# Division on coefficients, output bias in the rows' biases, and LayerNorm's factor and shift inside a gelu on features, between graph attention layers

## The reference, cut to what matters

```python
def _layer_norm(x, g, b):
    mu = jnp.mean(x, axis=-1, keepdims=True)
    var = jnp.var(x, axis=-1, keepdims=True)
    return g * (x - mu) / jnp.sqrt(var + 1e-05) + b

def _gatv2(h, src, dst, n, Wl, bl, Wr, br, att, bias):
    H, C = att.shape
    xl = (h @ Wl + bl).reshape(n, H, C)
    xr = (h @ Wr + br).reshape(n, H, C)
    x_i = xl[dst]
    x_j = xr[src]
    e = jax.nn.leaky_relu(x_i + x_j, NEG_SLOPE)
    logit = jnp.einsum('ehc,hc->eh', e, att)
    m = jax.ops.segment_max(logit, dst, num_segments=n)
    ex = jnp.exp(logit - m[dst])
    den = jax.ops.segment_sum(ex, dst, num_segments=n)
    alpha = ex / (den[dst] + 1e-16)
    out = jax.ops.segment_sum(alpha[..., None] * x_j, dst, num_segments=n)
    return out.reshape(n, H * C) + bias
...
for Wl, bl, Wr, br, att, bo, g, be in layers:
    h_new = jax.nn.gelu(_layer_norm(_gatv2(h, src, dst, n, Wl, bl, Wr, br, att, bo), g, be), approximate=False)
    h = h + h_new if h.shape == h_new.shape else h_new
out = h @ W_out + b_out
```

## Time and profile before

| what | value |
|---|---|
| median of 3 runs | 6894.73 us (6893.92 to 6904.86) |
| the profiled execution's own time | 6896.92 us |
| its span, first to last instruction | 6894.9 us |
| mean granted TensorE clock | 0.790 of full speed |
| PE busy | 4310.3 us, 63% |
| POOL busy | 4046.8 us, 59% |
| DVE busy | 3609.1 us, 52% |
| ACT busy | 1561.5 us, 23% |

### The profile page before, as it was taken

How to read it: one execution, slowest core, us unless ns; L and a number is a source line. 1 busy time by engine, 2 the same in 40 slices (tenths; PEclk the granted TensorE clock), 3 DMA queues, 4 the chain that set the end, 5 groups by cost and what they waited for, 6 DMA issues and landing times. The chain is left out here.

```text
span 6894.9 us, 131457 instructions
## 1 busy us (share of the span) xinstructions
PE 4310.3 (63%) x28719; PEld 3668.6 (53%) x28720; DVE 3609.1 (52%) x9059; ACT 1561.5 (23%) x3121; POOL 4046.8 (59%) x3272
## 2 busy tenths in 40 slices
PE   6768874666666636666665366666653656565664
PEld 5765333555555535555555365555553355555554
DVE  7888235455545565555555655555556244444445
ACT  4664100111111101111111011111111044444442
POOL 0100004888888548888884488888840078888883
PEclk9989986787778868888777688887876877787777
DMA  5753442666666526666665366666641311111111
GB/s 149 201 163 115 114 116 75 172 184 179 180 176 180 160 75 176 183 177 183 176 180 153 80 180 184 178 182 181 179 138 46 106 40 41 41 41 41 41 42 26
DMA packets 767773, 902.49 MB, mean 131 GB/s; under 512 B 278082, under 2 KB 543484, under 8 KB 767662
## 3 DMA queue, kind: packets, MB, share of 16 engines
q10 hardware_dynamic: 272511, 333.81, 16.8%
q1 hardware_dynamic: 234670, 326.01, 16.2%
q0 software_dynamic: 260480, 241.33, 15.3%
HBM read 654.18 MB, written 243.02 MB: 130 GB/s over the span
## 5 line engine op out<-in xcount | busy, mean ns | idle before, releaser
L484 POOL DMA_INDIRECT rows<-row_table,now x2400 | 2975.9, 1240 | 1646.2 <-issue 1588.9
L484 POOL DMA_INDIRECT rows<-node_table,now x800 | 1022.3, 1278 | 674.5 <-issue 668.5
L722 PE MATMUL zp<-parts,hot_t 125*125 x8100 | 755.2, 251 | 824.0 <-issue 570.6
L803 DVE SCALAR_TENSOR_TENSOR z<-zp,own 125x512 f32<-125x512 f32 x672 | 464.6, 691 | 1413.5 <-PE zp L725 1339.2
L722 PEld LDWEIGHTS zp<-parts,hot_t 125*125 125x125 bf16 x8100 | 698.0, 158 | 907.5 <-issue 903.0
L725 PE MATMUL zp<-rows,ident 125*125 x2700 | 941.4, 481 | 164.8 <-SPq L506 163.9
L736 PEld LDWEIGHTS sums<-values,hot 125*125 125x125 f32 x5376 | 877.4, 223 | 114.9 <-issue 42.7
L651 ACT CAST hot<-hot 125x500 f32<-125x500 bf16 x672 | 408.5, 608 | 2235.5 <-DMA hot<-hots 1262.6
L736 PE MATMUL sums<-values,hot 125*125 125x137 f32 x5376 | 879.5, 315 | 41.1 <-DVE values L815 36.4
L725 PEld LDWEIGHTS zp<-rows,ident 125*125 125x125 f32 x2700 | 553.8, 228 | 255.2 <-issue 178.8
L972 PE MATMUL turn<-ident,onehot 125*126 125x125 f32 x904 | 178.8, 333 | 515.0 <-DVE onehot L540 497.5
(11 more groups left out here) (414 smaller groups left out, 5047.6 us busy)
## 6 DMA issues: line engine op xcount, KB each, us to landing
back<-gathered ACTq DMA_DIRECT2D x624, 231.0 KB
gathered<-rows SPq DMA_DIRECT2D x600, 231.0 KB
hot_t<-hots_t ACTq DMA_DIRECT2D x678, 122.1 KB
hot<-hots ACTq DMA_DIRECT2D x672, 122.1 KB
counts<-pairs SPq DMA_DIRECT2D x75, 685.1 KB
rows<-row_table,now POOLq DMA_INDIRECT x2400
spread_slots<-slot_table POOLq DMA_DIRECT2D x56, 488.3 KB
hots_t<-hot_t SPq DMA_DIRECT2D x112, 218.8 KB
```

Source lines behind the costliest of these rows:

```text
L484: pool.indirect_dma_start(rows[:, q, j, :], None, table, bass.IndirectOffsetOnAxis(ap=now[:, half, lane + j:lane + j + 1], axis=0)).then_i ...
L722: pe.matmul(zp[:, p, j, 0:ROW], hot_t[:, q, j * P:(j + 1) * P], own[part], start=part == 0 and j % 2 == 0, stop=False, skip_group_check=True)
L803: dve.scalar_tensor_tensor(out=z[:, p, :, :], in0=zp[:, p, :, 0:D], scalar=0.0, in1=rows_of(own_att, HALF), op0=ALU.max, op1=ALU.mult).the ...
```

## The change

The functions `load`, `attention`, `linear_nodes` and the loops stay as they are. The change has four parts.

- The reciprocal of the denominator multiplies the two coefficients (`es`, 100 values a partition each) ahead of the scaling, not the result (3200 values a partition) behind it.
- The output bias is added to `xr`'s bias and subtracted from `xl`'s at the start of `attention_rows` (two DVE instructions of 125x128). The attention weights of a node sum to one, so its sum over rows carries the bias, and `xl + xr` in the logits is what it was. The bias comes as a new tile `late` with the layer's other loads.
- `normalize` and `to_features` become one block, `normalize_to_features`: DVE does (y - mean) * rstd in one pass, PE transposes each group of four windows when it is scaled, and ACT reads the PSUM bank with gelu, with the gain as per-partition scale and the shift as per-partition bias, since features are partitions now. In the first layer ACT writes `ft` itself; in the others it writes `grown`, and DVE adds it to `ft` group by group, two groups behind.
- `h` on nodes is gone as a tile. Gain and shift are loaded as columns (128 partitions x 4 bytes) instead of broadcasts; after the last layer `xr`'s memory serves as `h`.

The core of the diff:

```diff
+def normalize_to_features(nc, g, y, gain, shift, func, dst, onto=False):
...
+            def add_on(q):
+                dve.wait_ge(activated, q + 1)
+                dve.tensor_tensor(dst[:, part(q)], dst[:, part(q)], grown[:, part(q)], ALU.add)
...
+            link(dve.reciprocal(rstd[:, :], std[:, :]))
+            for q in range(GROUPS):
+                for w in windows(q):
+                    dve.tensor_scalar(y[:, w, :], y[:, w, :], moments[:, w, 0:1], rstd[:, w:w + 1], ALU.subtract, ALU.mult).then_inc(scaled, 1)
+                if onto and q >= 2:
+                    add_on(q - 2)
+            if onto:
+                for q in range(GROUPS - 2, GROUPS):
+                    add_on(q)
...
+            for q in range(GROUPS):
+                pe.wait_ge(scaled, windows(q)[-1] + 1)
+                for w in windows(q):
+                    ins = pe.transpose(bank[:, q, (w % 4) * P:(w % 4 + 1) * P], y[:, w, :], g.ident[0:P, 0:P])
+                ins.then_inc(turned, 1)
...
+            for q in range(GROUPS):
+                act.wait_ge(turned, q + 1)
+                act.activation(grown[:, part(q)], bank[:, q, 0:span(q)], func, bias=shift, scale=gain).then_inc(activated, 1)
...
+            link(dve.tensor_tensor(bias[:, 0, 0:D], bias[:, 0, 0:D], late[:, :], ALU.subtract))
+            link(dve.tensor_tensor(bias[:, 1, 0:D], bias[:, 1, 0:D], late[:, :], ALU.add))
...
+                (late[:, :], a[f"L1_gnn_bo{i}"].partition_broadcast(P))]
...
-                    link(dve.tensor_tensor(heads(xr[:, :, 0:D]), heads(xr[:, :, 0:D]), over(m[:, :, :]), ALU.mult))
-                    link(dve.tensor_tensor(xr[:, :, 0:D], xr[:, :, 0:D], rows_of(bo, WIN), ALU.add))
+                    for n in range(2):
+                        link(dve.tensor_tensor(es[:, :, n, :], es[:, :, n, :], m[:, :, :], ALU.mult))
...
-            def keep(dve, link):
-                if i == 0:
-                    link(dve.tensor_copy(h[:, :, :], xr[:, :, 0:D]))
-                else:
-                    link(dve.tensor_tensor(h[:, :, :], h[:, :, :], xr[:, :, 0:D], ALU.add))
-
-            normalize(nc, xr[:, :, 0:D], g.eps, gain=gain, shift=shift, func=ACT.Gelu, after=keep)
-            to_features(nc, g.ident, h, D, ft)
+            normalize_to_features(nc, g, xr[:, :, 0:D], norm[:, 0:1], norm[:, 1:2], ACT.Gelu, ft, onto=i > 0)
```

More of the change, by code:

```diff
@@ L305, in _ @@
                     act.activation(y[:, w:w + FIVE, :], y[:, w:w + FIVE, :], func).then_inc(activated, 1)
+def normalize_to_features(nc, g, y, gain, shift, func, dst, onto=False):
+    with Scope(nc) as sc:
+        stats = sc.sb("stats", [P, WIN, 6])
+        moments = sc.sb("moments", [P, WIN, 2])
+        std = sc.sb("std", [P, WIN])
+        rstd = sc.sb("rstd", [P, WIN])
+        grown = sc.sb("grown", [D, N]) if onto else dst
+        bank = sc.ps("bank", [128, GROUPS, 512])
+        names = ("step", "stats_ready", "moments_ready", "std_ready", "scaled", "turned", "activated")
+        step, stats_ready, moments_ready, std_ready, scaled, turned, activated = (sc.sem(x) for x in names)
+        block = sc.block()
+        part = lambda q: slice(4 * q * P, 4 * q * P + span(q))
+        @block.vector
+        def _(dve):
+            link = Link(dve, step)
+            def add_on(q):
+                dve.wait_ge(activated, q + 1)
+                dve.tensor_tensor(dst[:, part(q)], dst[:, part(q)], grown[:, part(q)], ALU.add)
+            for w in range(WIN):
+                dve.bn_stats(stats[:, w, :], y[:, w, :]).then_inc(stats_ready, 1)
+            dve.wait_ge(stats_ready, WIN)
+            for w in range(WIN):
+                dve.bn_aggr(moments[:, w, :], stats[:, w, :]).then_inc(moments_ready, 1)
+            dve.wait_ge(moments_ready, WIN)
+            dve.wait_ge(std_ready, 1)
+            link(dve.reciprocal(rstd[:, :], std[:, :]))
[7 more added lines that the diff above has]
+                    add_on(q)
+        @block.tensor
+        def _(pe):
+            for q in range(GROUPS):
[3 more added lines that the diff above has]
+                ins.then_inc(turned, 1)
+        @block.scalar
+        def _(act):
+            act.wait_ge(moments_ready, WIN)
+            act.activation(std[:, :], moments[:, :, 1], ACT.Sqrt, bias=g.eps[0:P, :]).then_inc(std_ready, 1)
+            for q in range(GROUPS):
+                act.wait_ge(turned, q + 1)
+                act.activation(grown[:, part(q)], bank[:, q, 0:span(q)], func, bias=shift, scale=gain).then_inc(activated, 1)
@@ L2010, in layer0, with attention_rows @@
         normalize(nc, x[:, :, :], g.eps, before=lambda dve, link: link(dve.tensor_tensor(x[:, :, :], x[:, :, :], cur[:, :, :], ALU.add)))
-def attention_rows(nc, g, i, k, ft, w, att_w, bias, own, table, xr, xl, loads):
+def attention_rows(nc, g, i, k, ft, w, att_w, bias, late, own, table, xr, xl, loads):
     per = 3
@@ L2072, in layer_loads @@
                 (att_w[:, :], a[f"L1_gnn_att{i}"].rearrange("h c -> (h c)").partition_broadcast(D)),
-                (bias[:, 0, 0:D], a[f"L1_gnn_bl{i}"].partition_broadcast(P)), (bias[:, 1, 0:D], a[f"L1_gnn_br{i}"].partition_broadcast(P))]
+                (bias[:, 0, 0:D], a[f"L1_gnn_bl{i}"].partition_broadcast(P)), (bias[:, 1, 0:D], a[f"L1_gnn_br{i}"].partition_broadcast(P)),
+                (late[:, :], a[f"L1_gnn_bo{i}"].partition_broadcast(P))]
     with Scope(nc) as sc:
-        h = sc.sb("h", [P, WIN, D])
         ft = sc.sb("ft", [128, N])
@@ L2083, in layer1 @@
         own = sc.sb("own", [P, D])
-        row = sc.sb("row", [P, 3, D])
+        late = sc.sb("late", [P, D])
+        norm = sc.sb("norm", [D, 2])
         ls = sc.sb("ls", [P, WIN, HEADS])
@@ L2098, in layer1 @@
             k = HID if i == 0 else D
-            rows = [(row[:, n, :], a[f"L1_gnn_{v}{i}"].partition_broadcast(P)) for n, v in enumerate(("bo", "g", "be"))]
-            bo, gain, shift = (row[:, n, :] for n in range(3))
-            attention_rows(nc, g, i, k, ft, w, att_w, bias, own[:, :], table, xr, xl, rows)
+            cols = [(norm[:, n:n + 1], column(a[f"L1_gnn_{v}{i}"])) for n, v in enumerate(("g", "be"))]
+            attention_rows(nc, g, i, k, ft, w, att_w, bias, late, own[:, :], table, xr, xl, cols)
             attention(nc, g, table, xl, xr, att_w[0:P, :], own[:, :], spill, ls)
@@ L2129, in _ @@
                     dve.wait_ge(exped, 1)
-                    link(dve.tensor_tensor(heads(xr[:, :, 0:D]), heads(xr[:, :, 0:D]), over(es[:, :, 0, :]), ALU.mult))
-                    link(dve.tensor_tensor(heads(g.acc[:, :, 0:D]), heads(g.acc[:, :, 0:D]), over(es[:, :, 1, :]), ALU.mult))
-                    link(dve.tensor_tensor(xr[:, :, 0:D], xr[:, :, 0:D], g.acc[:, :, 0:D], ALU.add))
                     link(dve.tensor_tensor(m[:, :, :], es[:, :, 1, :], g.acc[:, :, D:D + HEADS], ALU.mult))
```

8 lines of the change are left out of this document (6 added, 2 removed).

## The result

| | kernel before | changed kernel |
|---|---|---|
| median of 4 runs each | 6897.28 us (6893.92 to 6904.86) | 6853.16 us (6848.78 to 6855.49) |
| ratio | | 0.9934, 95% interval 0.9917 to 0.9951 |
| the profiled execution, and its span | 6896.92, 6894.9 us | 6855.44, 6853.7 us |
| mean granted TensorE clock | 0.790 | 0.794 |

The changed kernel is 44 us faster, where 57 were forecast. 6853.2 lies 1.2 us above the upper end of the forecast range. The forecast counted from 6894.7, the median of three executions; a fourth moved that median to 6897.3. 44.1 us less than 6894.7 would be 6850.6, inside the range.

What follows compares the result with a forecast made beforehand. DVE, busy almost without a gap between barriers in the parts between edge loops, was taken as the bound. Terms -19.4 + 1.9 + 0.4 - 15.4 - 13.5 - 13.3 + 2.0 = -57.3 from 6894.7 gave 6837.4 us, range 6829 to 6852.

Steps and rivals of the forecast that it cites:

- Division and bias: Block combining the sums: two large DVE instructions go, two small come, -19.4 us over three layers; bias instructions +1.9, load +0.4.
- One pass and gelu on features: First scaling to next block: 8.7, 11.1 and 11.1 us in the three layers, gains 15.4, 13.5 and 13.3 us.
- the rival *mode: Scaling pass reads one tensor and streams twice as fast: 5.2 us less, 6832.2 us; chance 0.04.
- The last additions: Second and third layer, additions of gelu results to `ft`: only the last ones wait, under 0.5 us.
- The clock: After spurts of transposes `linear_nodes` begins at PE's low clock level, +2.0 us; the two `attention_rows` 0.
- The rival *the clock: PE stays at the low level throughout `linear_nodes` and `attention_rows`: +11.8 us, 6849.2 us; chance 0.10.
- Lockstep: Normalisation, second and third layer: each group costs its whole chain of 3.4 us, +26 us, 6863 us; chance 0.03.
- slower gathers: Edge loops: moved `attention` tiles slow all 2400 gathers by 38 ns, +91 us, 6929 us; chance 0.03.
- no effect: Parts between loops: something else holds the barrier and the change saves nothing, 6894 us; chance 0.02.
- the loops over edges within 1 us of before: Sign to check: edge loops keep their length within 1 us; a change of several us would make the prediction wrong.
- theory C: Edge loops, posed for the follow-up runs: they lengthen whenever the parts are shorter, giving back 8 to 12 us.
- B: Edge loops, posed for the follow-up runs: they scatter by some us between executions, whatever the kernel, by either sign.

Runs made afterwards that it cites:

- c_after: The changed kernel again on another chip, quad number read as the lower 16 bits of its word; 7045.01 us, ratio 0.9932 to the kernel before.
- f_after: The changed kernel a third time, on the last chip, with the same 16-bit quad read; 7051.49 us, ratio 0.9932 to the kernel before.
- f_short_after: The changed kernel without its three long attention edge loops, two fills in their place; 2963.10 us, against 3014.56 for the kernel before cut likewise.
- d_warm: The changed kernel plus spare PE transposes in the holes between groups and at the start of each `attention_rows`; ratio 0.9934 to the kernel before.
- c_: Runs on one chip: control, changed kernel, changed kernel with tiles at old addresses, division-only edit; the kernel before took 7096.09 us there.
- d_: Runs on another chip: kernel before with only the bias edit (1.0002), changed kernel with spare transposes (0.9934) or with sums on POOL (0.9924).
- c_coeff: The kernel before with only the division moved to the coefficients; ratio 0.9993 to the kernel before, three parts 9.0 us less than the control.
- f_best: The changed kernel with next-layer sums prepared on POOL and three spare transposes behind groups 2 to 4 of later layers; 7047.84 us, ratio 0.9919.
- d_pool: The changed kernel with the next `attention_rows`' bias instructions, logit sums and scaled weights moved to POOL during normalisation; ratio 0.9924 to the kernel before.

## Why the prediction was right, and where not

From `some` behind a loop to the end of the part, in four profiles of the changed kernel's parts (`changed`, `c_after`, `f_after`, `f_short_after`), in us:

| step | forecast | before | found |
|---|---|---|---|
| block that combines the sums, each layer | -6.46 | 21.58 | 15.12, in all (-6.46) |
| first scaling to next block, 1st layer | 8.7 | 24.17 | 8.86, 8.41, 8.40, 8.40 |
| the same, 2nd layer | 11.1 | 24.57 | 11.21, 11.22, 11.21, 11.21 |
| the same, 3rd layer | 11.1 | 24.41 | 11.21, 11.22, 11.21, 11.21 |
| `linear_nodes` | +2.0 | 6.71 | 8.30, 8.60, 8.29, 9.46 (+1.6 to +2.8) |
| second and third `attention_rows` (first three profiles) | +0.65 each | 21.60, 20.29 | 22.37, 22.10; 21.63, 21.65; 21.58, 22.03 |

- **Division and bias: right.** The load stayed hidden. `late` was issued at 2418.08 + 0.34 and SP waited 3.8 us for it, so it was there near 2422, 8 us before DVE's last instruction ends (the first line is from SP's timeline, the second from its waits in that block):

```profile
2418.08 0.34 SPq L2175 DMA_DIRECT2D late<-in_L_gnn_bo  x1
...
SPq L103 <- DMA late<-in_L_gnn_bo: 3.8, 1, 3.8
```

  The two bias instructions take 0.32 us each. The column loads cost nothing visible.
- **One pass and gelu on features: right.** The tails came out 0.3 us short of the forecast or 0.15 over it in the first layer and 0.1 over it in the others. The two values of the first layer come from TensorE's clock: over the last transposes it was 0.50 in the changed kernel and 0.80 in `c_after`, and the last group's gelu takes 0.45 us and not 0.36. Of the two rules weighed, the first falls at this size: 25 instructions of L340 take 6.50 us, 0.26 each, about as long as the two-tensor form. "VectorE: DVE Perf Modes" of the Trainium skill, in "The perf-mode tier table", gives fp32 tensor_scalar twice the rate of tensor_tensor, for 2048 elements; with 128 elements the trace does not show it. So the rival *mode* is out. The other holds: L361 takes 767 ns. "ScalarE: Activation LUTs" of the Trainium skill, in "What ACT_TABLE_LOAD costs", has 93 ns for each pointer operand, which on top of the 677 ns of the row with one gives an estimate of 0.77 us; the trace agrees. My 0.7 was the row with one pointer.

```profile
L361 ACT ACTIVATE grown<-bank,norm x14: 449/767/768, 3794.5 to 5155.5; 128x500 f32<-128x500 f32 x12, 128x125 f32<-128x125 f32 x2
```

- **The last additions: a little off.** I expected less than 0.5 us of waiting; it was 0.55. Addition 5 started 10.02 us after the first scaling (3792.18 to 3802.20), where the working had 9.9: the gelu's 0.77 us in place of 0.7 is most of that. In `d_warm`, where a group's transposes take 0.65 us, the wait is gone and the distance is 10.76 us.
- **The clock: right mechanism, right size for `linear_nodes`, luck for `attention_rows`.** +2.0 for `linear_nodes` against +1.6 to +2.8. (The profile has 50 matmuls there, not the 25 of the prediction; the time it worked with is right.) The 0 for `attention_rows` was a difference of two numbers that each move. Before, the pair took 21.60 and 20.29 us in one execution and 20.43 and 22.11 in another; after, it is 21.6 to 22.4. The profiled pair shows +0.1 and +1.2 us beyond the bias instructions, and the latter is most of why the part between the second and third loop shrank by 18.0 us and not by 19.4. The rival *the clock* expected 11.8 us more than the sum; the profiled pair has 1.6 + 0.1 + 1.2 = 2.9 where the sum had 2.0, so it is out.
- **Lockstep, slower gathers, no effect: out.** No wait of a whole chain; gathers take 1239 and 1283 ns, against 1240 and 1278.
- **What failed: "the loops over edges within 1 us of before", and with it the upper end of the range.** The loops came out 1.8, 3.6 and 2.1 us longer, which touches the prediction's own sign of being wrong ("several us"), though the gathers are not slower. The terms for the three parts were -58.3 together and measured -57.0. The rest of the span moved by +16 where +1.0 was in the sum, and the range had no term for that. Three loops of 1300 us, a fourth edge loop and 1057 us of counting wander by several us each from execution to execution, as the count stage does between 1048 and 1063 us in my profiles. I had three runs, within 11 us, and allowed "a little" for them. The interval of the measured ratio, 0.9917 to 0.9951, is 12 us to either side; a range with such a term would have held the result.

**What stays open.** The whole kernels differ by 44, 51 and 46 us in three comparisons and by 51.5 without the loops, each below the 57 of the parts. Chance can do this, but a small loss outside of the parts can as well. The counting stage was 1052.7 us on average in six kernels without the full change (1048.0 to 1057.6) and 1057.7 in eight with it (1053.2 to 1063.1). The single values scatter by 4.0 and 3.4 us (standard deviations), so the difference of 5.0 has a standard error of 2.0: more than one would leave to chance, though its code is the same. On the chip of the `c_` runs it was 1050.2 and 1048.0 without against 1057.1 and 1061.4 with, on the last chip 1050.1 against 1055.7, 1063.1 and 1055.4; on the chip of the `d_` runs there is no such gap (1057.2 and 1053.2 against 1053.2 and 1055.8). With 5 us lost there and 1 in the other terms, the 57 of the parts would be 51 in the whole, which all these measurements allow. No run tells a cause from chance here. The stage `load, ft` is 0.3 us longer in most of the changed kernels, which is the one more load, and about 1.5 us in three of them. For the loops themselves theory C has no clear support: both kernels have a profile on two chips, with 3892 against 3900 us on the first and 4101 against 4096 on the next, where `c_coeff` had 4078. B fits, but a loss of a few us in the loops is not excluded.

## What to carry to other kernels

Between two barriers with DVE busy all through, count its instructions: in the block that combines the sums removing them paid to 0.1 us, and each edit alone gave its term within 2 us, the rest being TensorE's clock. When the stages that an edit does not touch are a hundred times as long as the gain, give their scatter a term of its own in the range (13.5 us here), and judge small edits by the stage's own timeline, or in a kernel that leaves the long stages out. Work in spurts on PE made what follows start at half clock here. A few spare transposes, in the holes and ahead of the next matmuls, gave 7.3 us of the parts, and work moved to an idle POOL 7.5; the whole times do not show either.

## What I had not expected of the hardware

- The same loop with the same instructions took 1295 to 1302 us on the first chip, 1339 to 1394 on two others and 1444 to 1469 on another, at 172, 160 and 152 GB/s in the second loop. The remaining edge loop hardly differed: from its first gather to its last it took 1260 to 1270 us in all fourteen profiles. No run shows why.
- Matmuls with 32 rows of contraction stayed at 1.2 GHz for all of their 22.36 us, with PE busy throughout and 16 spare transposes of 128x128 ahead. Those with 128 rows went at 2.4 GHz from the first (granted clock 1.00) behind 5.9 us of transposes and 16 spare ones, or, in `f_best`, 1.35 and 1.50 us behind transposes without long holes; `d_pool` shows that the latter is not certain (13.03 us in place of 11.49).
- POOL's small tensor instructions (16 of them, 0.2 to 0.7 us each) are quick enough to be hidden under 7.5 us of DVE's statistics; in the profile they did not slow DVE, whose 25 statistics took 4.93 us as before.
